# A retention stage whose score matmuls are issued ahead of the output matmuls, whose state product closes each output group, and whose queries are spread over head columns by ScalarE instead of VectorE

## What is computed

```python
Q = jnp.einsum('bld,hde->bhle', x, Wq)
K = jnp.einsum('bld,hde->bhle', x, Wk)
V = jnp.einsum('bld,hde->bhle', x, Wv)
Dm = _decay_mask(Lq)          # gamma_h ** (l - m) for l >= m, else 0
scores = jnp.einsum('bhle,bhme->bhlm', Q, K) * Dm[None] / math.sqrt(HEAD_DIM)
out = jnp.einsum('bhlm,bhme->bhle', scores, V)
...                           # normalised over (8 dims of a head, all 1024 positions)
return combined @ Wout
```

## Time and profile before

| what | value |
|---|---|
| median of 3 runs | 1945.7 us (1944.68 to 1946.38) |
| the profiled execution: its time, and its span | 1935.43 us, 1933.3 us |
| TensorE, weight loads, VectorE, ScalarE, GpSimd busy, whole span | 87%, 49%, 76%, 49%, 18% |
| mean granted TensorE clock, whole span | 0.942 |
| retention: first decay to last chunk's first decay | 1563.65 to 1750.18 us |
| in it: TensorE waits for VectorE's decays before output matmuls (L1609) | 14.5 us in 68 waits |
| in it: VectorE waits for scores before a decay (L1744) | 9.0 us in 13 waits |
| in it: VectorE waits for the update (L1758) | 12.5 us in 17 waits |

### The profile page before, as it was taken

The page is one execution under the profiler, slowest core; times in us unless marked ns, Lnnn a source line. Parts: engine busy times, 40 slices in busy tenths (PEclk is TensorE's granted clock), DMA queues, the critical chain, the costliest instruction groups (busy, mean ns, idle before and its releaser), DMA issues. The chain is left out here.

```text
span 1933.3 us, 30370 instructions
## 1 busy us (share of the span) xinstructions
PE 1676.1 (87%) x10673; PEld 952.5 (49%) x10673; DVE 1468.5 (76%) x2501; ACT 947.0 (49%) x1798; POOL 355.7 (18%) x698
## 2 busy tenths in 40 slices
PE   5899999789999999999998899999865588885565
PEld 5788888421111111111113688888744455553354
DVE  5755555889999999999973765557688768886886
ACT  3223324368888888888886323232344311112442
POOL 5310013540000010000003200100113232333111
PEclk9999999889999999999999999999888889997888
DMA  3000001120001100110100100000000000000000
GB/s 121 1 1 0 0 0 48 51 83 21 22 28 32 35 21 22 42 33 21 37 8 9 30 24 0 0 0 1 1 0 1 1 1 2 1 1 1 1 22 22
DMA packets 25296, 35.84 MB, mean 19 GB/s; under 512 B 5808, under 2 KB 19696, under 8 KB 24672
## 3 DMA queue, kind: packets, MB, share of 16 engines
q1 hardware_dynamic: 25184, 34.38, 5.9%
HBM read 22.57 MB, written 8.78 MB: 16 GB/s over the span
## 5 line engine op out<-in xcount | busy, mean ns | idle before, releaser
L1086 DVE TENSOR_REDUCE neg_half<-PS 128x2 f32<-128x1024 f32 x512 | 601.4, 1220 | 38.6 <-PE PS L928 23.6
L1023 ACT ACTIVATE probs<-PS 128x512 f32<-128x512 f32 x1024 | 528.9, 603 | 112.3 <-PE PS L939 112.2
L502 ACT ACTIVATE shared<-PS 128x512 f32<-128x512 f32 x256 | 152.6, 597 | 374.6 <-PE PS L411 362.6
L598 DVE TENSOR_TENSOR shared<-shared,PS 128x512 f32<-128x512 f32 x256 | 177.8, 718 | 155.9 <-ACT shared L502 154.1
L939 PE MATMUL PS<-qk_all 51*128 51x512 bf16 x1024 | 279.4, 387 | 17.0 <-ACT probs L1023 12.1
L951 PE MATMUL PS<-probs,Vg 128*32 128x512 f32 x2048 | 274.5, 608 | 0.1
L420 PEld LDWEIGHTS PS<-wd,shared 128*128 128x128 f32 x2048 | 249.0, 192 | 11.1 <-issue 0.5
L420 PE MATMUL PS<-wd,shared 128*128 128x128 f32 x2048 | 250.3, 276 | 0.0
L939 PEld LDWEIGHTS PS<-qk_all 51*128 51x128 bf16 x1024 | 71.7, 93 | 337.1 <-ACT probs L1023 318.6
L928 PE MATMUL PS<-qk_all 48*128 48x512 bf16 x1024 | 194.1, 391 | 17.5 <-DVE neg_half L1086 15.1
L606 DVE SCALAR_TENSOR_TENSOR x<-PS,gates,x 128x128 f32 (+1 forms) x512 | 146.8, 368 | 69.4 <-PE PS L420 69.4
(11 more groups left out here) (209 smaller groups left out, 2133.5 us busy)
## 6 DMA issues: line engine op xcount, KB each, us to landing
split<-qk_all SPq DMA_DIRECT2D x16, 384.0 KB, 3.3
qk_all<-split SPq DMA_DIRECT2D x64, 96.0 KB
qk_all<-split SPq DMA_DIRECT2D x64, 64.0 KB
qk_all<-split SPq DMA_DIRECT2D x64, 32.0 KB
shared<-OTs SPq DMA_DIRECT2D x60, 32.0 KB
probs<-in_ret_const SPq DMA_DIRECT2D x1, 1538.5 KB, 6.7
qk_all<-negT SPq DMA_DIRECT2D x96, 4.0 KB, 1.7
SC<-inverse SPq DMA_DIRECT2D x3, 512.0 KB, 5.1
```

The lines of the kernel that those rows point to most:

```text
L502: act.activation(sg[:, f, :], bank(f), ACT.Silu).then_inc(s["silu"], 1)
L598: dve.tensor_tensor(h[:, FCH * (e % 2) + f, :], sg[:, f, :], bank(2 + f), ALU.mult).then_inc(s["h"], 1)
L1023: act.activation(probs[:, n % 2, STRIPS * strip + pair, :], bank(RING_AT + use % RING), ACT.Exp, scale=ATT_SCALE).then_inc(s["exped"], 1)
L1086: dve.tensor_reduce(neg_half[m % 2][:, i % 2, :, at], bank(use_bank(i, m), 2).rearrange("p (s w) -> p s w", s=STRIPS), AX.X, ALU.max, nega ...
```

## The change

1. On TensorE a turn k is now: scores of k + 1, outputs of k (the 16 matmuls first, the state product last), update of k, projection of k + 3, transpose of k + 4. The scores of k + 1 wait for the decays of k bank by bank; the outputs wait for all four decays of k at once.
2. `qm` is made by ScalarE: four ACTIVATEs (Identity, with a column of `k_row` as scale), which read the projection in PSUM, directly after the copy to `pj`. The scores wait for the new semaphore `qm`, no longer for `masked`. VectorE keeps `qd` and `kd`.
3. ScalarE's order in a turn: take out the outputs of k, copy and spread projection k + 3, copy the transpose of k + 4. Projections are now three chunks ahead.
4. VectorE's order in a turn: four decays of k, the new state of k - 1, `masks` of k + 2, the work beside, `norm` of k + 5.
5. `qd`, `kd` and `pj` have three buffers (two before), `pd` two (one before). The loops over sequences are written out on every engine. `ln_finish` of the second half of a sequence moves on GpSimd from c = 7 to the next sequence's c = 0, behind `vm`.

The core of the diff (left out: the old bodies, which stand above, unchanged work that moved into functions, and slices written without registers):

```diff
-        rxn, rxT, qd, kd = (carve(2 * P).rearrange("p (u w) -> p u w", u=2) for _ in range(4))
-        pj = carve(8 * P).rearrange("p (u w) -> p u w", u=2)
+        rxn, rxT = (carve(2 * P).rearrange("p (u w) -> p u w", u=2) for _ in range(2))
+        qd, kd = (carve(3 * P).rearrange("p (u w) -> p u w", u=3) for _ in range(2))
+        pj = carve(12 * P).rearrange("p (u w) -> p u w", u=3)
...
-        pd = shared[:, 0:HG * JH * P].rearrange("p (g j l) -> p g j l", g=HG, j=JH)
+        pd = shared[:, :].rearrange("p (u g j l) -> p u g j l", u=2, g=HG, j=JH)
...
-            def transposeT(k, u):
+            def transposeT(k):
                 pe.wait_ge(s["xn"], k + 1)
-                wait(pe, s["pj"], k - 1)
-                pe.transpose(bank(4 + u)[:, 0:P], rxn[:, u, :], ident[:, :]).then_inc(s["xT_ps"], 1)
-
-            def project(k, u):
+                wait(pe, s["qm"], k - 1)
+                pe.transpose(bank(4 + k % 2)[:, 0:P], rxn[:, k % 2, :], ident[:, :]).then_inc(s["xT_ps"], 1)
...
+            def score(k):
+                pe.wait_ge(s["qm"], k + 1)
+                for g in range(HG):
+                    wait(pe, s["decayed"], HG * (k - 1) + g + 1)
+                    pe.matmul(bank(g), kT[g * 32:(g + 1) * 32, k % 3, :], qm[g * 32:(g + 1) * 32, k % 2, :, :],
+                              start=True, stop=True).then_inc(s["scoreT"], 1)
+
+            def outputs(k):
+                b, c = k // BT, k % BT
+                wait(pe, s["o"], k)
+                pe.wait_ge(s["vm"], k + 1)
+                pe.wait_ge(s["decayed"], HG * (k + 1))
+                for j in range(JH):
+                    for g in range(HG):
+                        last = pe.matmul(bank(6)[g * 32:(g + 1) * 32, 0:P], vm[:, k % 2, j, g * 32:(g + 1) * 32],
+                                         pd[:, k % 2, g, j, :], start=(j == 0), stop=(c == 0 and j == JH - 1),
+                                         skip_group_check=True)
+                if c > 0:
+                    pe.wait_ge(s["masked"], k + 1)
+                    pe.wait_ge(s["state"], b * STATES + c)
+                    last = pe.matmul(bank(6)[:, 0:P], state[:, :], qd[:, k % 3, :], start=False, stop=True, skip_group_check=True)
+                last.then_inc(s["o_ps"], 1)
...
+            transposeT(0)
+            transposeT(1)
+            project(0)
+            project(1)
+            transposeT(2)
+            project(2)
+            transposeT(3)
+            score(0)
+            for k in range(CHUNKS_ALL):
+                if k + 1 < CHUNKS_ALL:
+                    score(k + 1)
+                outputs(k)
+                update(k)
+                if k + 3 < CHUNKS_ALL:
+                    project(k + 3)
+                if k + 4 < CHUNKS_ALL:
+                    transposeT(k + 4)
...
-            def chunk_in(k, u):
+            def turned(k):
                 act.wait_ge(s["xT_ps"], k + 1)
-                act.activation(rxT[:, u, :], bank(4 + u)[:, 0:P], ACT.Copy).then_inc(s["xT"], 1)
+                act.activation(rxT[:, k % 2, :], bank(4 + k % 2)[:, 0:P], ACT.Copy).then_inc(s["xT"], 1)
+
+            def projected(k):
                 act.wait_ge(s["proj"], k + 1)
-                act.activation(pj[:, u, :], bank(4 + u), ACT.Copy).then_inc(s["pj"], 1)
-
-            def batch(b, beside, final):
-                for c in range(BT):
-                    k, u = b * BT + c, c % 2
-                    if not (final and c == BT - 1):
-                        chunk_in(k + 1, 1 - u)
-                    act.wait_ge(s["o_ps"], k + 1)
-                    act.activation(ro[:, bass.ds(outputs_of(b) + c * P, P)], bank(6)[:, 0:P], ACT.Copy).then_inc(s["o"], 1)
-
-            chunk_in(0, 0)
-            batches(act, batch)
+                act.activation(pj[:, k % 3, :], bank(4 + k % 2), ACT.Copy).then_inc(s["pj"], 1)
+                wait(act, s["scoreT"], HG * (k - 1))
+                for j in range(JH):
+                    last = act.activation(qm[:, k % 2, j, :], bank(4 + k % 2)[:, 0:P], ACT.Identity, scale=k_row[:, j:j + 1])
+                last.then_inc(s["qm"], 1)
+
+            act.wait_ge(ld["ret"], 32)
+            turned(0)
+            turned(1)
+            projected(0)
+            projected(1)
+            turned(2)
+            projected(2)
+            turned(3)
+            for k in range(CHUNKS_ALL):
+                b, c = k // BT, k % BT
+                act.wait_ge(s["o_ps"], k + 1)
+                act.activation(ro[:, outputs_of(b) + c * P:outputs_of(b) + (c + 1) * P], bank(6)[:, 0:P], ACT.Copy).then_inc(s["o"], 1)
+                if k + 3 < CHUNKS_ALL:
+                    projected(k + 3)
+                if k + 4 < CHUNKS_ALL:
+                    turned(k + 4)
...
+                if b > 0 and c == BT - 2:
+                    ln_finish(pool, 5, (b - 1) * 2)
+                if b > 1 and c == 0:
+                    ln_finish(pool, 5, (b - 2) * 2 + 1)
...
-            def masks(k, u):
+            def masks(k):
                 dve.wait_ge(s["pj"], k + 1)
-                o = pj[:, u, :]
-                wait(dve, s["scoreT"], HG * (k - 1))
-                dve.tensor_tensor(qm[:, u, :, :], o[:, 0:P].unsqueeze(1).to_broadcast([P, JH, P]),
-                                  k_row.unsqueeze(2).to_broadcast([P, JH, P]), ALU.mult)
-                wait(dve, s["o_ps"], k - 1)
-                dve.tensor_tensor(qd[:, u, :], o[:, 0:P], k_qd, ALU.mult)
-                dve.tensor_tensor(kd[:, u, :], o[:, 2 * P:3 * P], k_kd, ALU.mult).then_inc(s["masked"], 1)
+                o = pj[:, k % 3, :]
+                wait(dve, s["o_ps"], k - 2)
+                dve.tensor_tensor(qd[:, k % 3, :], o[:, 0:P], k_qd, ALU.mult)
+                dve.tensor_tensor(kd[:, k % 3, :], o[:, 2 * P:3 * P], k_kd, ALU.mult).then_inc(s["masked"], 1)
...
+            norm(0)
+            norm(1)
+            norm(2)
+            masks(0)
+            norm(3)
+            masks(1)
+            norm(4)
+            for k in range(CHUNKS_ALL):
+                b, c = k // BT, k % BT
+                wait(dve, s["o_ps"], k - 1)
+                for g in range(HG):
+                    decay(k, g)
+                if k > 0:
+                    new_state(k - 1)
+                if b > 0 and c == 3:
+                    group_affine(b - 1)
+                if k + 2 < CHUNKS_ALL:
+                    masks(k + 2)
+                if b > 0 and c == 0:
+                    group_moments(b - 1)
+                if b > 0 and c == BT - 1:
+                    dve.wait_ge(s["added"], len(Y_CHUNKS) * b)
+                    ln_stats(dve, (b - 1) * 2 + 1)
+                if k + 5 < CHUNKS_ALL:
+                    norm(k + 5)
```

More of the change, by code:

```diff
@@ L1625, in ret_pe, with update @@
-            transposeT(0, 0)
-            project(0, 0)
-            batches(pe, batch)
+            def update(k):
+                b, c = k // BT, k % BT
+                if c == BT - 1:
+                    return
+                pe.wait_ge(s["masked"], k + 1)
+                if c == 0:
+                    wait(pe, s["state"], b * STATES)
+                if b > 0 and c == 1:
+                    average(b - 1)
+                if b > 0 and c in Y_CHUNKS:
+                    pe.wait_ge(s["cn"], b)
+                    for j in range(2):
+                        t = 2 * (c - Y_CHUNKS[0]) + j
+                        pe.matmul(bank(7)[:, (1 + j) * P:(2 + j) * P], cn[:, t * P:(t + 1) * P], wout[:, :], start=True, stop=True)
+                pe.matmul(bank(7)[:, 0:P], kd[:, k % 3, :], vs[:, k % 3, :], start=True, stop=True).then_inc(s["update"], 1)
@@ L1775, in ret_dve, with new_state @@
[L1775 to L1780 removed]
+            def new_state(k):
+                b, c = k // BT, k % BT
+                if c == BT - 1:
+                    return
+                dve.wait_ge(s["update"], b * STATES + c + 1)
+                if c == 0:
+                    dve.tensor_tensor(state[:, :], bank(7)[:, 0:P], k_blk, ALU.mult).then_inc(s["state"], 1)
+                    return
+                own(dve.tensor_tensor(rtmp[:, :], bank(7)[:, 0:P], k_blk, ALU.mult))
+                if b > 0 and c == 1:
+                    group_variance(b - 1)
+                if b > 0 and c in Y_CHUNKS:
+                    at = c - Y_CHUNKS[0]
+                    if at == 2:
+                        dve.wait_ge(s["added"], len(Y_CHUNKS) * (b - 1) + at)
+                    xs = x[:, (b - 1) * BT + 2 * at:(b - 1) * BT + 2 * at + 2, :].rearrange("p t c -> p (t c)")
+                    dve.tensor_tensor(xs, bank(7)[:, P:3 * P], xs, ALU.add).then_inc(s["added"], 1)
+                dve.wait_ge(s["o_ps"], k + 1)
+                dve.scalar_tensor_tensor(state[:, :], state[:, :], k_g128, rtmp[:, :], ALU.mult,
+                                         ALU.add).then_inc(s["state"], 1)
+                if b > 0 and c == Y_CHUNKS[2]:
+                    ln_stats(dve, (b - 1) * 2)
```

141 lines of the change are left out of this document (28 added, 113 removed).

## The result

The changed kernel takes 1912.4 us (median of 4, 1911.18 to 1916.54) against 1945.8 us (median of 4, 1944.68 to 1946.38): the ratio is 0.9834, with a 95% interval of 0.9819 to 0.9849, 33.4 us faster. The forecast was 1904.7 us.

A forecast was written before the change was run, and what follows sets the result against it. A ring of scores, decays and `qm` was taken to bound the kernel. Opening it gives -49.7, less 3.4 start, 3 half clock, 2 hand-overs and 0.3 end: -41.0 us, from 1945.7 to 1904.7, range 1897 to 1928.

The forecast's parts named there:

- One ring closes: Before, in the first sequence: scores, decays, `qm`, `qd` and `kd` on VectorE, next scores; 5.29 us a turn, nothing overlapping.
- TensorE 3.91 a turn: TensorE's work in one new turn sums to 3.91 us and sets the first sequence, 31.3 us.
- VectorE in the later sequences plus 1 us each: VectorE's work without `qm` sets sequences two to four, with 1 us added each: 35.7, 36.5 and 33.3 us.
- Hand-overs 2: New hand-overs between engines give back 2 us, from between 0 and 4.3, most falling beside longer work.
- The start, 3.4: Three projections and two `qm` ahead of the first decay make it 3.4 us later.
- ScalarE, costed at nothing: `qm` on ScalarE costs nothing: the ring through ScalarE, 3.3 us, is 0.6 shorter than TensorE's turn.
- The rival of a ring through ScalarE: ScalarE's copies and slower `qm` bind, with an unforeseen wait of 0.5 us every turn: -21 us; chance 0.09.
- Slower, and nothing moves: Two rivals: TensorE at half clock, 2004 us if in all turns, chance 0.04; another wait keeps the old turn, 0.02.
- The signs: Expected profile: first-sequence decays 3.9 to 4.1 us apart, later 4.4 to 4.8, clock 0.95 or more; also signs of being wrong.
- State last, +0.3: At the end, the state product following the outputs gives back 0.3 us.
- that part moves to where `vm` has slack: On GpSimd, one `ln_finish` half moves to where `vm` has slack; the other stays at c = 6, about 0.5 us late.
- GpSimd in VectorE's way: `vm` blocks one VectorE instruction in each of 24 later turns: 12 to 30 us; 20 gives 1925; chance 0.13.

## Why the prediction was right, and what it had wrong

The mechanism held in its second half: with no ring left, the turn is the work of the longest engine, TensorE in the first sequence and VectorE in the later ones. The first half, which ring was to be opened, was incomplete.

- *"One ring closes"*, and *"The projection and most output matmuls fit inside the ring's VectorE part"*. The last 26 output records, the update and the transpose don't: they stand between the last decay and the next scores and close a second ring of 5.29 us. The ring that the prediction named gives nothing when it is opened alone. That the change opened the other too, by putting the scores ahead of the outputs, is luck as far as the argument for the change goes; the sum didn't suffer, since it took the new turn from the engines' work, and the path that it followed for the new order holds.
- *TensorE 3.91 a turn.* Measured 3.76. Projection, update and transpose take 1.30 instead of 1.52, scores and state 0.07 more. 8 x 0.15 = 1.2 us, to the good.
- *VectorE in the later sequences plus 1 us each.* 105.5 forecast for the three. With GpSimd out of the way they take 103.8. The allowance that I distrusted was good, and `norm` on ScalarE shows that VectorE does set these turns.
- *Hand-overs 2.* Not found: the stage of the run with `ln_finish` last is 136.8, against 141.8 forecast with them.
- *The half-clock turn, 3.* 33.0 - 8 x 3.76 = 2.9.
- *The start, 3.4.* Measured 1.15: projection and scores ran at full clock, which I had priced at half.
- *ScalarE, costed at nothing.* The four operations of a `qm` take 1.13 us, where I had 1.19, and the cover was 0.8. The rival of a ring through ScalarE didn't come.
- *VectorE over 93% busy in sequences two to four.* 98, 91 and 98%; the 91 is the half-clock turn's.
- *Slower, and nothing moves.* One turn of the later 24 ran at half clock, where half of them would have been needed. Two slips in that rival change nothing: 56 more than now is 2002 and not 2004, and with half of the turns at half clock the granted clock, which is a mean over time, would be about 0.69 and not 0.76.
- *The signs.* Turns of 3.76 in the first sequence, not 3.9 to 4.1; of 3.25 to 8.32 later, where 4.4 to 4.8 was asked for; a granted clock of 0.90 to 1.00 by window, where 0.95 or more was. Two of the signs of being wrong showed, each once: a half-clock stretch inside the later stage, and outputs that wait for `vm`.
- *State last, +0.3.* The experiment has it at 0.15 a turn to the good.
- **The term that was mis-sized is GpSimd's**: "that part moves to where `vm` has slack. The other half stays at c = 6, about 0.5 us late; it lies beside the scores." `vm` came 2.2 us late (3.0 after a turn's first decay; 0.8 in the run with `ln_finish` last, 1642.06 against 1641.22). I followed it only to the scores, and not to what VectorE does at that time, nor to the last chunk, where no slack is left. Priced at 0, it costs 14.9 by the medians. In the profiled executions 6.6 in four turns and 2.1 at the last outputs follow from the late `vm`. The rest, 2.9 for a half-clock turn and 3.5 behind the last outputs, went with it in this pair of executions; by what way is not shown.

This is my rival of "GpSimd in VectorE's way", which came true in part. I had given it one blocked instruction in each of 24 turns or none. It strikes where `vm` slides off the decays: 11 of VectorE's small instructions take 1.25 to 1.38 us in retention, against 6 with `ln_finish` last. Each costs about 1.0 to 1.1, nearly the whole of `vm`. Before it was 4, and there `qm` bore most of it: 15 of its 32 took 1.04 to 1.41 us instead of 0.68. (Moving `qm` to ScalarE took it out of `vm`'s way, a gain that the prediction counted without naming it.) The Trainium skill ("SBUF — State Buffer", Who interferes with whom) has a VectorE instruction with two SBUF inputs blocked fully beside GpSimd's reads; by that rule 1.38 for a 128x128 is what is to be expected, and the trace agrees. The 1.11 of the earlier trace rows, which I had read as a milder form, was a `qm` that started 0.7 us into its `vm`.

What stays open: why TensorE's clock fell at 1656.4 in the changed kernel. With `ln_finish` last the later windows stand at 1.00, but that is one execution: the run with `norm` on ScalarE and the two with half of the outputs are built on it and have one or two such stretches in the second to fourth sequence (turns of 7.18, 7.54 and 7.42 instead of 5.46 or less). With the state first, `qm` made twice or on VectorE, and with a second `vm`, there are three or more, mostly behind turns in which TensorE stood idle (0.86 us ahead of the fall at 1656.4). No run changed such waits alone.

## What to carry to other kernels

Before opening a ring, look for a second one of the same length: with the ring through `qm` open and the other closed the turn stayed at 5.29 us, twice, and with both open it fell to 3.76. When an engine counts as busy without a gap, look whether its rows are as long as its work before calling it the bound. An engine that is half idle isn't free: see where in the turn its long instructions fall, and take side work ahead of them out of the loop. When an instruction comes late, follow the delay to every engine that is busy at that time, not only to the one that waits for it.

## What the runs showed of the hardware

- `vm` holds more than VectorE's instructions with two large SBUF inputs: `norm`, a TENSOR_SCALAR with one 128x128 input and two columns, took 1.36 us beside it instead of 0.33 (1652.47), and a SCALAR_TENSOR_TENSOR on 128x4 elements 1.25 (1612.83). The decays, which read PSUM, keep 2.47 for four beside it, and a BATCH_NORM_STATS2 on 128x128 in SBUF keeps its 0.27 to 0.28 (1724.70).
- A half-clock turn cost 2.9 us here: 8.32 against 5.46 for the same turn with `ln_finish` last, and 2.9 in the first sequence (33.0 less 8 turns of 3.76).
- ScalarE's Identity with a scale column on 128x128 took 1.12 to 1.14 us for four from PSUM, in all 32 groups and at either clock of TensorE, against 1.28 for four from SBUF in the earlier trace rows.
